# Second attention of a one-core transformer kernel: long tiles turned in two instructions, their buffer handed back in two halves

## The reference, cut to what matters

```python
g = NH // NKV                                   # 32 // 8 = 4 query heads share one key head
kf = jnp.repeat(kf, g, axis=1)
v = jnp.repeat(v, g, axis=1)
scores = jnp.einsum('bhqd,bhkd->bhqk', q, kf) / jnp.sqrt(jnp.asarray(HD, dt))
scores = jnp.where(causal, scores, jnp.finfo(dt).min)
attn = jax.nn.softmax(scores, axis=-1)
out = jnp.einsum('bhqk,bhkd->bhqd', attn, v)
```

## Time and profile before

| | |
|---|---|
| median of 3 runs | 2586.15 us (2585.09 to 2587.84) |
| the profiled execution's own time | 2579.9 us |
| its span, first to last instruction | 2578.1 us |
| mean granted clock of TensorE | 0.969 |
| second attention, first maximum to last reciprocal | 1151.9 to 1970.2 us |
| one unit in the steady state | 50.87 us (1561.87 to 1612.74 us) |

### The profile page before, as it was taken

One profiled execution on the slowest core, in us unless ns is written; L12 is line 12 of the kernel. 1 busy time (PEld: TensorE's weight loads), 2 busy tenths in 40 slices (PEclk: granted clock), 3 DMA queues, 4 the chain that ended last, 5 costly groups with the idle time before them and its releaser, 6 DMA issues. The chain is left out here.

```text
span 2578.1 us, 52965 instructions
## 1 busy us (share of the span) xinstructions
PE 2266.5 (88%) x21584; PEld 1566.7 (61%) x21584; DVE 1449.1 (56%) x2103; ACT 868.2 (34%) x1804; POOL 425.4 (16%) x374
## 2 busy tenths in 40 slices
PE   4988987899999799968888888888986997999997
PEld 3565654677777578843444444444444886788886
DVE  4433423333322534538888888888885333676665
ACT  4232221322222230015555555555554221211114
POOL 0000000121122115430111111111111000322221
PEclk9999999899999899988999999999999998999999
DMA  4011010700000653332333433343333661211111
GB/s 141 1 65 64 2 49 24 248 23 18 25 8 0 230 183 118 120 117 65 91 99 78 109 93 97 83 116 85 92 87 98 224 229 51 56 31 28 33 37 65
DMA packets 169261, 217.90 MB, mean 85 GB/s; under 512 B 36624, under 2 KB 108368, under 8 KB 165360
## 3 DMA queue, kind: packets, MB, share of 16 engines
q1 hardware_dynamic: 168208, 213.62, 27.3%
q10 hardware_dynamic: 864, 1.57, 0.2%
HBM read 143.76 MB, written 71.37 MB: 83 GB/s over the span
## 5 line engine op out<-in xcount | busy, mean ns | idle before, releaser
L1380 ACT ACTIVATE a_prob<-ps,a_nmax 128x256 f32<-128x256 f32 (+7 forms) x512 | 377.0, 739 | 365.0 <-DVE a_nmax L1408 230.4
L1490 PE MATMUL ps<-a_kt,a_q 64*128 64x512 f32 (+5 forms) x1536 | 381.1, 537 | 104.7 <-ACT a_prob L1380 84.4
L1408 DVE TENSOR_REDUCE a_nmax<-ps 128x1 f32<-128x1024 f32 (+3 forms) x256 | 256.5, 1002 | 103.5 <-PE ps L1490 103.0
L1490 PEld LDWEIGHTS ps<-a_kt,a_q 64*128 64x128 f32 x1536 | 143.7, 194 | 202.2 <-ACT a_prob L1380 124.9
L1422 DVE STREAM_TRANSPOSE a_pt_long<-a_prob 128x1024 f32<-128x1024 f32 (+3 forms) x256 | 257.9, 1022 | 0.0
L1504 PE MATMUL ps<-a_pt_long,a_v 32*64 32x256 f32 (+3 forms) x7808 | 227.1, 342 | 0.4 <-DVE a_pt_long L1422 0.2
L1504 PEld LDWEIGHTS ps<-a_pt_long,a_v 32*64 32x64 f32 x7808 | 153.3, 131 | 100.8 <-issue 75.0
L1457 POOL TENSOR_TENSOR a_o<-a_left 128x256 f32<-128x256 f32 x128 | 90.4, 728 | 610.8 <-ACT a_left L1390 610.8
L50 PE MATMUL ps<-f_w_hi,f_hT_hi 128*128 128x512 f32 x432 | 168.5, 390 | 3.6 <-POOL f_hT_lo L1801 3.6
L51 PE MATMUL ps<-f_w_lo,f_hT_hi 128*128 128x512 f32 x432 | 168.6, 390 | 0.0
L52 PE MATMUL ps<-f_w_hi,f_hT_lo 128*128 128x512 f32 x432 | 168.0, 389 | 0.0
(11 more groups left out here) (212 smaller groups left out, 4353.4 us busy)
## 6 DMA issues: line engine op xcount, KB each, us to landing
a_q<-scratch_QT SPq DMA_DIRECT2D x512, 64.0 KB, 2.1
scratch_QT<-k_qo SPq DMA_DIRECT2D x64, 256.0 KB, 2.3
a_v<-scratch_V SPq DMA_DIRECT2D x64, 256.0 KB, 4.7
scratch_OT<-a_o SPq DMA_DIRECT2D x32, 512.0 KB, 3.2
o_of<-scratch_OT SPq DMA_DIRECT2D x32, 512.0 KB, 4.5
f_packed<-in_packed SPq DMA_DIRECT2D x11, 768.0 KB, 6.0
a_kt<-scratch_KT SPq DMA_DIRECT2D x128, 64.0 KB, 4.0
f_scale<-in_scale SPq DMA_DIRECT2D x11, 384.0 KB, 6.1
```

What stands on the lines that cost most here:

```text
L1380: last = nc.scalar.activation(prob[:, n % PRING, s].rearrange("p (a w) -> p a w", w=w), SC[n % 2][:, a, 0:w], ACT.Exp, bias=nmax[:, n % 4, ...
L1408: nc.vector.tensor_reduce(nmax[:, n % 4, 0:1], SC[n % 2][:, :, 0:width(0, t)], AX.XY, ALU.max, negate=True).then_inc(maxed, 1)
L1490: last = pe.matmul(sc[:, a, 0:w], q[r, slot, heads[a * hf], :], kt[r, b, keys], start=not masked, stop=True, skip_group_check=True)
```

## The change

Each long tile's turn becomes two instructions. FRONT turns key blocks 0 to 15 (512 columns), BACK turns the rest: 512, 384, 256 or 128 columns for t = 7, 6, 5, 4. FRONT of tile i stands at step i + 2 for all 16 long tiles. BACK stands where the whole turn stood, but for tile 8, which goes from step 11 to step 10. A new semaphore, `half_valued`, is raised by PE after value block 15 of the long half; FRONT of tile 0 waits for it, and BACK of tile 0 waits for `valued` as the whole turn did. Blocks 15 to 17 belong to step 23. The short tiles stay as they are. All that waited for a tile's turn now waits for its BACK. With it, at each step the FRONT is listed ahead of the BACKs.

```diff
--- before.py
+++ after.py
@@ -1218,8 +1218,14 @@
 FIRST = (4, 0)
 BLOCKS = (32, 16)
 
-TURNS = {5: [0], 6: [1], 7: [2, 3], 8: [4], 9: [5, 6], 10: [7], 11: [8, 9]}
-TURNS.update({i + 2: [i] for i in range(10, USTEPS)})
+FRONT, BACK, WHOLE = range(3)
+TURNS = {i + 2: [(i, FRONT)] for i in range(LONG)}
+for r, back in {5: (0,), 6: (1,), 7: (2, 3), 8: (4,), 9: (5, 6), 10: (7, 8)}.items():
+    TURNS[r] += [(i, BACK) for i in back]
+for i in range(9, LONG):
+    TURNS[i + 2] += [(i, BACK)]
+TURNS.update({i + 2: [(i, WHOLE)] for i in range(LONG, USTEPS)})
+MIDDLE = 16
 
 LONG_VALUES = {18 + i: range(3 * i, 3 * i + 3) for i in range(10)}
 LONG_VALUES[28] = range(30, 32)
@@ -1291,6 +1297,7 @@
         scored, maxed, exped, turned = sem("scored"), sem("maxed"), sem("exped"), sem("turned")
         inverted, spread_out, valued = sem("inverted"), sem("spread_out"), sem("valued")
         evicted, o_done, o_stored = sem("evicted"), sem("o_done"), sem("o_stored")
+        half_valued = sem("half_valued")
 
         def width(hf, t):
             return (t + 1) * P // 2 if hf == 0 else (t + 1) * P
@@ -1298,8 +1305,11 @@
         turn_order = []
         for n in range(NSTEPS + LATEST):
             for u, r in at_step(n, TURNS):
-                turn_order += [u * USTEPS + i for i in TURNS[r]]
-        turn_number = {n: i + 1 for i, n in enumerate(turn_order)}
+                turn_order += [(u * USTEPS + i, part) for i, part in TURNS[r]]
+        turn_number = {turn: i + 1 for i, turn in enumerate(turn_order)}
+
+        def last_turn(n):
+            return turn_number[n, BACK if n % USTEPS < LONG else WHOLE]
 
         with nc.Block() as block:
             @block.sync
@@ -1371,7 +1381,7 @@
                         wait(act, inverted, 2 * unit + hf - 1)
                     act.wait_ge(maxed, n + 1)
                     if n >= PRING:
-                        act.wait_ge(turned, turn_number[n - PRING])
+                        act.wait_ge(turned, last_turn(n - PRING))
                     w = width(hf, t)
                     for i, h in enumerate(heads):
                         a = slice(0, 2) if hf == 0 else slice(i, i + 1)
@@ -1411,15 +1421,18 @@
                         nc.vector.tensor_reduce(nmax[:, n % 4, :], SC[n % 2][:, :, 0:width(1, t)], AX.X, ALU.max,
                                                 negate=True).then_inc(maxed, 1)
 
-                def turn(n):
+                def turn(n, part):
                     unit, hf, t, heads = place(n)
-                    if n % USTEPS in (0, LONG):
+                    if n % USTEPS == 0 and part == FRONT:
+                        wait(dve, half_valued, unit)
+                    elif n % USTEPS in (0, LONG):
                         wait(dve, valued, 2 * unit + hf - 1)
                     dve.wait_ge(exped, n + 1)
                     blocks = 4 * (t + 1)
+                    lo, hi = {FRONT: (0, MIDDLE), BACK: (MIDDLE, blocks), WHOLE: (0, blocks)}[part]
                     for i, h in enumerate(heads):
-                        src = prob[:, n % PRING, i * blocks * 32:(i + 1) * blocks * 32]
-                        last = nc.vector.transpose(pt[hf][:, 0:blocks, h, t - FIRST[hf], :],
+                        src = prob[:, n % PRING, (i * blocks + lo) * 32:(i * blocks + hi) * 32]
+                        last = nc.vector.transpose(pt[hf][:, lo:hi, h, t - FIRST[hf], :],
                                                    src.rearrange("p (j k) -> p j k", k=32))
                     last.then_inc(turned, 1)
 
@@ -1433,8 +1446,8 @@
                     if n < NSTEPS:
                         maxima(n)
                     for u, r in at_step(n, TURNS):
-                        for i in TURNS[r]:
-                            turn(u * USTEPS + i)
+                        for i, part in TURNS[r]:
+                            turn(u * USTEPS + i, part)
                     for u, r in at_step(n, (LONG + 2, USTEPS + 2)):
                         invert(u, r == USTEPS + 2)
 
@@ -1501,8 +1514,11 @@
                                 continue
                             rows = slice(32 * i, 32 * i + 32)
                             out = PV[i][c * HD1:(c + 1) * HD1, 0:256].rearrange("p (s t q) -> p s t q", s=2, t=4)
-                            pe.matmul(out[:, :, a - t0:4, :], v[rows, b, j, :], pt[hf][rows, j, c::2, a - t0:4, :],
-                                      start=j == 0, stop=j == BLOCKS[hf] - 1, skip_group_check=True)
+                            last = pe.matmul(out[:, :, a - t0:4, :], v[rows, b, j, :],
+                                             pt[hf][rows, j, c::2, a - t0:4, :],
+                                             start=j == 0, stop=j == BLOCKS[hf] - 1, skip_group_check=True)
+                    if hf == 0 and j == MIDDLE - 1:
+                        last.then_inc(half_valued, 1)
 
                 def denominators(half):
 
@@ -1517,7 +1533,7 @@
                 def values(unit, hf, blocks):
                     half = 2 * unit + hf
                     if blocks[0] == 0:
-                        pe.wait_ge(turned, max(turn_number[unit * USTEPS + i]
+                        pe.wait_ge(turned, max(last_turn(unit * USTEPS + i)
                                                for i in (range(LONG) if hf == 0 else range(LONG, USTEPS))))
                         wait(pe, evicted, 4 * half)
                         if hf == 0:
```

## The result

| | before | after |
|---|---|---|
| median of 4 runs each | 2585.62 us | 2567.49 us (2564.28 to 2570.70) |
| ratio, with its 95% interval | | 0.9934 [0.9922, 0.9947] |
| span of the profiled execution | 2578.1 us | 2562.5 us |
| one steady unit of the second attention | 50.87 us | 49.93 us |

The change makes the kernel 18.1 us faster by the medians, 15.6 by the two profiled spans.

A forecast was written before the change was run, and what follows sets the result against it. DVE's full queue bounds the middle of each second-attention unit, PE the rest. Saving 1.60 less 0.88, taken as 0.75 us a unit, fifteen units plus the first give 11.8: 2586.15 to 2574.3 us, range 2569.5 to 2581.5.

The forecast's parts named there:

- What bounds each stretch: Second attention unit: PE bounds steps 0 to 4, DVE's full queue runs to the turn of tile 15, then PE.
- rival 1: Steps 2 to 4: the three FRONTs cost PE 0.1 us each, gain 0.45 a unit, 2579 us; chance 0.13.
- rival 3: Steps 5 to 15: the score loop or PE already paces them; at most 0.25 us a unit, 2582 us; chance 0.06.
- Rival 4: Evener steps hand scores over earlier and the step 16 wait vanishes: 0.95 us a unit, 2571 us; chance 0.06.
- What was moved out: FRONTs of tiles 0 to 2 leave DVE's full stretch for steps 2 to 4: 1536 columns, 1.60 us a unit.
- 11 x 0.08 = 0.88 us a unit: DVE, steps 5 to 17: 13 added turns, two of them free, the other 11 at 0.08 us fixed cost each.
- sum step by step: Steps 5 to 13 added up: 18.96 us against 19.87, 0.91 less by step 14; 0.77 after steps 16 and 17.
- bound of 0.06: Lower bound for an added DVE turn's fixed cost, from 1024 and 512 columns: 11 x 0.06 = 0.66 us a unit.
- range for the likeliest case: The forecast's own range, 0.65 to 0.9 us saved a unit: 2571 to 2577 us; chance of the forecast 0.70.
- The first unit: First unit of the second attention: loses 0.22 us at the tighter step 2 and gains 0.5.
- Rival 2: DVE, steps 5 to 17: fixed 0.15 us an instruction paid in full; 2592.6 us, slower; chance 0.05.
- DVE busy 2.4 us more a unit: Sign that the forecast is right: DVE's busy time up by 16 x 0.15 us a unit, by recorded durations.

The follow-up runs named there:

- Doubling the FRONTs: Changed kernel plus a spare turn of 512 columns ahead of each FRONT of tiles 0, 1 and 2; 2582.18 us (one run).
- evened kernel with three split tiles: Against the kernel before: only tiles 0 to 2 split, whole turns as early as their exponentials allow; 2560.37 us, ratio 0.9908.
- Split in place: Against the kernel before: all 16 long turns split into FRONT and BACK, nothing moved; 2599.56 us, ratio 1.0066.
- FRONTs in two: Changed kernel with the FRONTs of tiles 3 to 11 each as two turns of 256 columns; 2575.08 us (one run).
- second timing: The changed kernel timed once more, unaltered, against the kernel before; 2569.12 us against 2584.55, ratio 0.9939.
- kernel with three split tiles: Against the kernel before: only tiles 0 to 2 split, all other turns whole at their old steps; 2579.60 us, ratio 0.9982.
- four early FRONTs: Against the kernel before: only tiles 0 to 3 split, FRONTs at steps 1 to 4, other turns whole and evened; 2551.88 us, ratio 0.9886.

## Why the prediction was right and wrong

**What bounds each stretch** was right. Steps 0 to 4 kept their 10.51 us with three more turns in them, the middle stretch lost time, and the path left DVE again at the turn of tile 15. Doubling the FRONTs showed that the cover is real and nearly used up; rival 1, that it leaks, is out, and so is rival 3: in an undisturbed unit no maxima of steps 6 to 15 wait. Of the margins, 0.03 and 0.25 us were forecast before the maxima of steps 4 and 5; none and 0.16 are recorded.

**Rival 4 had the right number and the wrong reason.** It named 0.95 us a unit, at a chance of 0.06, from evener steps and a vanishing wait at step 16. DVE's recorded idle time before those maxima did vanish, but steps 14 and 15 still take 3.10 us, so it gave nothing; the gain came from the price of the turns.

**What was moved out** was priced right: 1536 columns, 1.60 us. The evened kernel with three split tiles, which adds no instruction to the full stretch, measures just this.

**The step that failed is the term "11 x 0.08 = 0.88 us a unit" for the added turns.** Split in place and FRONTs in two both measure 0.06. Nine of the added turns stand in steps 5 to 13 and cost 0.53, so 1.60 - 0.53 = 1.07 less, against 1.06 measured for the middle stretch; the two in steps 14 and 15 were free, as forecast (those steps keep their 3.10 us); the two in 16 and 17 cost 0.12 where 0.14 was forecast. Together 0.94 a unit in place of 0.75; the sum step by step has the same fault, with 0.91 by step 14 where 1.06 is measured. The pair of 512 columns gave 0.61 as a mean of two distances that are not alike: 0.63 for the turn behind maxima, 0.59 for the turn behind a turn. An added turn is of the second kind, and 0.59 less 512 columns at 1.04 ns leaves 0.06 fixed. The pair of 128 columns gave the other kind, and slightly misread: its second turn starts 1563.24 - 1563.01 = 0.23 after the first, not 0.21, since the 284 ns taken off is the mean of both and the second is recorded with 0.27:

```profile
1563.24 0.27 DVE L1422 STREAM_TRANSPOSE a_pt_short<-a_prob 128x128 f32<-128x128 f32 x1
```

The bound of 0.06 that the prediction worked out below its choice was the right value, and would have given 0.94. The range for the likeliest case stopped at 0.9 all the same.

**The clock was left out of the sum.** 15 units at 0.94 are 14.1 us. That alone would have put the median at about 2572, inside the range. So the mis-sized price alone doesn't account for a median 2 us below the range, and the second timing's 15.4 us would have lain inside it. The rest, 1 to 4 us by the two timings, most likely lies in units that TensorE's clock disturbs: 6.2 us of excess on average in three profiles of before, 3.2 in two of after. That is not shown. The prediction read the clock in its windows of one undisturbed unit, where it is 1.00, and never asked how many of the units are disturbed; it thought of the clock only as a small chance of a slower kernel. The other experiments show that this can weigh more than the whole change: 16 us in the kernel with three split tiles.

The first unit was forecast to gain 0.5. Its profiles read 50.7, 53.5 and 50.6 us before, 51.1 and 51.7 after; a low clock around the start of the stage moves it by more than that, so this term stays open.

**Rival 2**, the fixed part exposed, is out by a factor of two and a half. The Trainium skill ("VectorE: DVE Perf Modes", the section on the TRN2 errata) has a fixed cost of some 150 cycles, exposed between instructions. That does not hold for these turns: their recorded durations carry 0.15 us beside the columns (686 ns for 512 columns), but one more turn in a full queue costs 0.06.

Of the signs to look for, "DVE busy 2.4 us more a unit" was wrong as well: it is 44.54 against 43.61, 0.93 more. Busy time counts the overlap of two instructions once, so what an added turn adds to it in a full queue is again the distance and not the duration.

## What to carry to other kernels

Where one engine's queue is full, price an added instruction by the distance that one more of its kind adds to a row of them (three against two), not by an average or by the recorded duration. A buffer handed back in halves pays by what can be done early under other work: split only as many pieces as fit there (in the undisturbed unit four split tiles gained 2.13 us where sixteen gained 0.94), and keep the rest of the queue even. Look at the granted clock over all repetitions of a stage and not in one clean one: in the kernel with three split tiles its falls took back more than half of what the schedule gained.

## What the runs showed of the hardware

- Turns of 32x32 blocks on DVE overlap the next instruction by some 0.08 us: of 512 columns, a turn is recorded with 0.67 us behind another turn, and the next instruction starts 0.59 us after it. Behind maxima a turn takes about 0.03 us more (0.62 to 0.63 from start to start).
- TensorE's granted clock fell in step with the program. In the kernel with three split tiles it was at half in 11 of 14 units, ten of them of 51.1 us, and in the one followed, from step 12 to 14; in the one with four early FRONTs in every second unit through two thirds of the stage. Before the falls PE had idle times of 0.45 to 1.33 us between scores; PE's work was the same in both. Undisturbed units have the same idle times, so these go with the falls but do not bring on each.
- Twenty small matmuls a unit, 0.9 us of PE time that nothing uses, went with the end of all five falls in the steady units of the kernel with four early FRONTs (one profile each), and made it faster by 4 us by the medians. The same filler in the changed kernel gained nothing, so this is at most a cure for a place that one has found, not a rule.
